# Norm factors by logarithm and exponential on ScalarE in place of GpSimd's power, and six buffers of routed rows for four

## What is computed

```python
def _layernorm(x, axis=-1, eps=1e-05):
    m = jnp.mean(x, axis=axis, keepdims=True)
    v = jnp.var(x, axis=axis, keepdims=True)
    return (x - m) / jnp.sqrt(v + eps)

x = _layernorm(x + attention(x, Wq, Wk, Wv, Wo, bo))   # 16 heads of 8, softmax
x = _layernorm(x + retention(x, ctx, ctx))             # decayed causal scores, rotated queries and keys, no softmax
x = _layernorm(x + experts(x, gate, w1, w2, w3))       # 8 experts of width 512, the two best by a softmax, silu(g) * u
```

## Time and profile before

| what | value |
|---|---|
| time, median of 3 runs | 1004.99 us (1000.88 to 1008.09) |
| the profiled execution | 1007.5 us |
| its span, first to last instruction | 1005.7 us |
| busy: PE, DVE, POOL, ACT | 804.7, 790.3, 652.6, 613.4 us |
| TensorE clock granted, mean | 0.915 |

### The profile page before, as it was taken

The page is one execution under the profiler, slowest core; times in us unless marked ns, Lnnn a source line. Parts: engine busy times, 40 slices in busy tenths (PEclk is TensorE's granted clock), DMA queues, the critical chain, the costliest instruction groups (busy, mean ns, idle before and its releaser), DMA issues.

```text
span 1005.7 us, 34508 instructions
## 1 busy us (share of the span) xinstructions
PE 804.7 (80%) x11940; PEld 603.2 (60%) x11940; DVE 790.3 (79%) x2155; ACT 613.4 (61%) x1416; POOL 652.6 (65%) x738
## 2 busy tenths in 40 slices
PE   1667799989999899898868660999999999999500
PEld 1345465656656556656544430799999999999500
DVE  4797799988999988998846644688888888888475
ACT  1133566768767777676666851676667666766355
POOL 0349767799999999998996456245444544454443
PEclk9788799999999999999987965899999999999855
DMA  9312222123232232221212004222222222222176
GB/s 307 81 29 54 40 48 50 42 62 70 51 71 62 54 74 52 61 58 42 63 39 62 23 22 91 58 61 66 63 62 61 66 63 61 62 65 58 53 252 226
DMA packets 145300, 72.55 MB, mean 72 GB/s; under 512 B 75024, under 2 KB 134544, under 8 KB 145136
## 3 DMA queue, kind: packets, MB, share of 16 engines
q1 hardware_dynamic: 124800, 40.43, 17.4%
q0 software_dynamic: 8640, 17.84, 5.4%
q10 hardware_dynamic: 11696, 12.08, 3.8%
HBM read 41.98 MB, written 28.34 MB: 70 GB/s over the span
## 4 chain that ended last, share of the span: by engine, by line
PE 38%; POOL 32%; issue 12%; DVE 3%; DMA 3%; ACT 2%; POOLq 0%; SPq 0%; ACTq 0%; DVEq 0%
POOL prod_ev L1536 17%; POOL routed_rows L1553 11%; PE QKV L773 9%; PE ST L773 9%; PE XT L801 6%; PE SC L801 5%; POOL rs L1516 3%; PE YY L589 2%; DMA prod_ev<-token_halves 2%; PE SC L560 1%; PE YY L791 1%; PE TR L791 1%; PE TR L606 1%; DMA routed_rows<-xe,pos 1%; PE TR L603 1%
## 5 line engine op out<-in xcount | busy, mean ns | idle before, releaser
L1536 POOL TENSOR_TENSOR prod_ev<-e_sb,q_v 128x512 f32<-128x512 f32 x256 | 300.2, 1206 | 70.5 <-PE YY L589 35.6
L1585 POOL DMA_INDIRECT token_halves<-w_new,tok_i x142 | 137.8, 971 | 32.5 <-issue 22.2
L1553 POOL DMA_INDIRECT routed_rows<-xe,pos x128 | 129.6, 1013 | 30.6 <-issue 29.9
L1151 DVE TENSOR_TENSOR prod_qk<-q_v,QKV 128x2048 f32<-128x2048 f32 x64 | 144.7, 2273 | 4.5 <-ACT q_v L870 4.5
L1438 DVE TENSOR_TENSOR prod_ev<-prod_qk,prod_ev 128x1024 f16<-128x1024 f32 x71 | 87.0, 1226 | 56.0 <-ACT prod_ev L1028 56.0
L1028 ACT CAST prod_ev<-prod_qk 128x1024 f16<-128x1024 f32 x71 | 74.2, 1045 | 76.0 <-DVE prod_qk L1464 51.4
L773 PE MATMUL QKV<-k_t,w_hl 128*128 128x256 f16 x852 | 116.8, 274 | 0.1
L773 PE MATMUL ST<-k_t,w_hl 128*128 128x256 f16 x852 | 116.7, 273 | 0.0
L409 POOL TENSOR_TENSOR marks<-half_c 128x1 f32<-128x1 f32 x103 | 19.9, 193 | 142.2 <-DVE w_new L1454 142.0
L1464 DVE SCALAR_TENSOR_TENSOR prod_qk<-ST,hid_scale,prod_qk 128x512 f32<-128x512 f32 x142 | 99.6, 744 | 2.3 <-ACT prod_qk L1037 2.3
L1037 ACT ACTIVATE prod_qk<-QKV,silu_scale 128x512 f32<-128x512 f32 x142 | 96.1, 678 | 8.6 <-PE QKV L773 4.6
(11 more groups left out here) (169 smaller groups left out, 1695.3 us busy)
## 6 DMA issues: line engine op xcount, KB each, us to landing
w_new<-routed_rows SPq DMA_DIRECT2D x71, 130.0 KB
prod_ev<-token_halves SPq DMA_DIRECT2D x16, 512.0 KB, 5.1
x_sb<-x SPq DMA_DIRECT2D x32, 128.0 KB, 3.0
x_res<-x SPq DMA_DIRECT2D x128, 32.0 KB
head_rows<-o_n SPq DMA_DIRECT2D x32, 128.0 KB
o_t<-head_rows SPq DMA_DIRECT2D x64, 64.0 KB
ctx_sb<-ctx SPq DMA_DIRECT2D x32, 128.0 KB, 2.7
out<-prod_qk ACTq DMA_DIRECT2D x16, 256.0 KB, 4.0
```

Source lines behind the costliest of these rows:

```text
L1151: eng.tensor_tensor(prod_qk[:, u, :, :].rearrange("p d (i j) -> p d i j", j=NH), q.unsqueeze(3).to_broadcast([P, HD, NH, NH]), k.unsqueeze ...
L1536: ins = eng.tensor_tensor(prod_ev[:, u, q, :, :, 0:HD], e_sb[:, it.slot(2), u, 64 * q:64 * q + 64].rearrange("p (i j) -> p j i", j=4).unsq ...
L1553: eng.indirect_dma_start(out=xs, out_offset=bass.IndirectOffsetOnAxis(ap=pos[:, r, 2 * u + k:2 * u + k + 1], axis=0), in_=xe[:, r, u, k, : ...
L1585: eng.indirect_dma_start(out=halves, out_offset=bass.IndirectOffsetOnAxis(ap=tok_i[:, s, u:u + 1], axis=0), in_=yw[:, s, u, :], in_offset= ...
```

## The change

- `one_over_std` moves from POOL to ACT. POOL's power and product go (L1516, L1527). ACT does three things in their place, between `row_ids(13)` and `blocks(9)`: ve = Ln(variance + eps), with eps as the bias, for 4 numbers a partition; rs = Exp(-0.5 * ve); and four one-column copies nb = nm * rs (each with a column of rs as its scale). Each of the three waits for the one before.
- DVE's `variances` loses its second instruction (variance + eps); nm now raises `nm_ready`, for which Ln waits.
- At the head of ACT's program, the activation table that holds both Ln and Exp is loaded.
- `xe` and the semaphores of the scatters have six homes (XE_RING) for four. `second_norm` and `gate_weights` wait for the scatter six duos back. `positions` still waits for the one four duos back, since `pos` keeps four buffers.

```diff
+XE_RING = 6
+def wait_row_ring(item, sems, back):
+    if item.off - back >= 0:
+        item.eng.wait_ge(sems[(item.off - back) % XE_RING], 64 * ((item.off - back) // XE_RING + 1))
...
-        xe = sb("xe", [RING, 2, 2, ROW])
+        xe = sb("xe", [XE_RING, 2, 2, ROW])
...
+            eng.preload_act_table_set("natural_log_exp_and_others")
             eng.wait_ge(tab_in, 16)
...
+            def one_over_std(c, d):
+
+                slot = norm_slot(c, d)
+                wait_norms(c, d, nm_ready)
+                eng.activation(ve[:, slot, :, :], mv[:, slot, :, :, 1], ACT.Ln, bias=eps_c[:, 0:1]).then_inc(ve_ready, 1)
+                wait_norms(c, d, ve_ready)
+                eng.activation(rs[:, slot, :, :].rearrange("p k u -> p (k u)"), ve[:, slot, :, :].rearrange("p k u -> p (k u)"),
+                               ACT.Exp, scale=-0.5).then_inc(rs_ready, 1)
+                wait_norms(c, d, rs_ready)
+                for k in range(2):
+                    for u in range(2):
+                        ins = eng.activation(nb[:, slot, k, u:u + 1], nm[:, slot, k, u:u + 1], ACT.Copy,
+                                             scale=rs[:, slot, k, u:u + 1])
+                ins.then_inc(nb_ready, 1)
...
                 wait(it, nb_ready, -NORM_GAP)
-                wait_ring(it, routed_out, RING, 64)
+                wait_row_ring(it, routed_out, XE_RING)
...
                 if it := at(13):
                     row_ids(it)
+                c, d = at(8), at(8 + NORM_GAP)
+                if c or d:
+                    one_over_std(c, d)
                 if it := at(9):
                     blocks(it)
...
-                eng.tensor_scalar(nm[:, slot, :, :], mv[:, slot, :, :, 0], -1.0, None, ALU.mult)
-                eng.tensor_scalar(ve[:, slot, :, :], mv[:, slot, :, :, 1], EPS, None, ALU.add).then_inc(ve_ready, 1)
+                eng.tensor_scalar(nm[:, slot, :, :], mv[:, slot, :, :, 0], -1.0, None, ALU.mult).then_inc(nm_ready, 1)
...
             def positions(it):
                 wait(it, posw_ready)
-                wait_ring(it, routed_out, RING, 64)
+                wait_row_ring(it, routed_out, RING)
...
-                eng.tensor_tensor(rs[:, slot, :, :].rearrange("p k u -> p (k u)"),
-                                  ve[:, slot, :, :].rearrange("p k u -> p (k u)"), half_c[:, 0:4], ALU.pow).then_inc(rs_ready, 1)
...
-                eng.tensor_tensor(nb[:, slot, :, :].rearrange("p k u -> p (k u)"), nm[:, slot, :, :].rearrange("p k u -> p (k u)"),
-                                  rs[:, slot, :, :].rearrange("p k u -> p (k u)"), ALU.mult).then_inc(nb_ready, 1)
...
                 if it := at(11):
                     scatter(it, 0)
-                c, d = at(5), at(5 + NORM_GAP)
-                if c or d:
-                    one_over_std(c, d)
-                c, d = at(5), at(5 + NORM_GAP)
-                if c or d:
-                    norm_shift(c, d)
                 if it := at(1):
                     weighted(it, 1, 0)
```

More of the change, by code:

```diff
@@ L377, in build @@
         ev_ready = [sem(f"ev_ready{u}") for u in range(2)]
-        ve_ready, rs_ready = sem("ve_ready"), sem("rs_ready")
-        x_in, ctx_in, routed_out = (ring_sem(n) for n in ("x_in", "ctx_in", "routed_out"))
+        nm_ready, ve_ready, rs_ready = sem("nm_ready"), sem("ve_ready"), sem("rs_ready")
+        x_in, ctx_in = (ring_sem(n) for n in ("x_in", "ctx_in"))
+        routed_out = [sem(f"routed_out{i}") for i in range(XE_RING)]
         y_in = ring_sem("y_in")
@@ L489, in _ @@
                               pad_rows[:, 2 * n:2 * n + 2, :]).then_inc(blank_out, 16)
-            for r in range(RING):
-                eng.wait_ge(routed_out[r], 64 * n_duo // RING)
+            for r in range(XE_RING):
+                eng.wait_ge(routed_out[r], 64 * ((n_duo - r + XE_RING - 1) // XE_RING))
             eng.wait_ge(blank_out, 16 + 16 * n_exp)
@@ L677, in rows_across @@
                 for u in range(2):
-                    mm = eng.transpose(X2T[:, P * u:P * u + P], xe[:, it.slot(RING), u, 0, 0:P], ident)
+                    mm = eng.transpose(X2T[:, P * u:P * u + P], xe[:, it.slot(XE_RING), u, 0, 0:P], ident)
                 mm.then_inc(x2t_done, 1)
@@ L853, in row_ids @@
                 wait(it, w1_ready)
-                eng.copy(xe[:, it.slot(RING), :, :, P + 1],
+                eng.copy(xe[:, it.slot(XE_RING), :, :, P + 1],
                                 const("ids")[:, bass.ds(it.number() * 4, 4)].rearrange("p (u k) -> p u k", k=2)
@@ L944, in second_norm @@
             def second_norm(it):
-                s, r, m = it.slot(2), it.slot(RING), norm_slot(None, it)
+                s, r, m = it.slot(2), it.slot(XE_RING), norm_slot(None, it)
                 wait(it, nb_ready, -NORM_GAP)
-                wait_ring(it, routed_out, RING, 64)
+                wait_row_ring(it, routed_out, XE_RING)
                 for u in range(2):
@@ L1286, in gate_weights @@
                 wait(it, dn_ready)
-                wait_ring(it, routed_out, RING, 64)
-                eng.reciprocal(xe[:, it.slot(RING), :, :, P], dn[:, it.slot(2), :, :]).then_inc(w1_ready, 1)
+                wait_row_ring(it, routed_out, XE_RING)
+                eng.reciprocal(xe[:, it.slot(XE_RING), :, :, P], dn[:, it.slot(2), :, :]).then_inc(w1_ready, 1)
             def places(it):
@@ L1544, in scatter @@
             def scatter(it, u):
-                r = it.slot(RING)
+                r, x = it.slot(RING), it.slot(XE_RING)
                 if u == 0:
@@ L1553, in scatter @@
                     eng.indirect_dma_start(out=xs, out_offset=bass.IndirectOffsetOnAxis(ap=pos[:, r, 2 * u + k:2 * u + k + 1], axis=0),
-                                           in_=xe[:, r, u, k, :], in_offset=None).then_inc(routed_out[r], 16)
+                                           in_=xe[:, x, u, k, :], in_offset=None).then_inc(routed_out[x], 16)
             def step(at):
```

## The result

The changed kernel took 1026.81 us at the median of 4 runs (1024.13 to 1029.21), the kernel before 1006.54 over 4 runs (1000.88 to 1010.2): ratio 1.0206, interval 1.0149 to 1.0262. The forecast was 972 in a range of 960 to 994, so it was wrong in sign. The profiled execution took 1024.13 us with a span of 1022.2, against 1005.7 before.

The account below looks back on a forecast made before the run. POOL was taken as the bound, 15.52 us in its best steps, with PE and DVE close behind. Gains of 22 (middle), 5 (fill), 3 (drain) and 3.3 (stage end) made 33.3 us, from 1004.99 to 972; range 960 to 994.

Parts of the forecast that it names:

- Where the stall goes: Middle steps: xq_a would fall among POOL's scatters, not its products, so its 0.97 us stall would be mostly gone.
- POOL's phase: Middle steps, counted from m_neg's end: POOL's products start at 1.4 us and its pair between the scatters at 8.6.
- It mends itself: Middle steps: if the stall returns, DVE and PE slow down, POOL gets ahead by the difference, and its pair ends sooner.
- Rival 3: Middle steps: one_hot and xq_a meet POOL's six products, 2.2 us more, a step of 16.4; 1016 us, chance 0.05.
- ACT's new work: ACT ahead of the first norm: Ln, Exp and four copies take 1.4 us, bounds 1.2 to 2.6, hidden by 1.66 idle.
- The fill: Stage A before 198.85: stalls of DVE's xq_a and one_hot go, gaining 5 us, bounds 0 and 9.
- The end: Stage A behind 512.80: 3 us from two more homes, 3.3 from last scatters no longer held behind the power.
- The step without a collision: Middle of stage A: 14.6 us a step for 15.70, bounds 14.3 and 15.2, gaining 22 us over 20 steps.
- rival 1: Middle steps: the collision at xq_a stays, a step of 15.2 and no gain in the fill; 989 us, chance 0.17.
- rival 2: ACT's six instructions cost 2.6 us, each drained before the next, a step of 15.4; 1000 us, chance 0.06.
- rival 4: ACT's tables for Ln and Exp replace each other, two loads of 1.28 us a step; 1023 us, chance 0.02.
- the rule on two-input instructions: POOL shares SBUF interfaces with DVE, with contention for two SBUF inputs; taken as giving no way to say which step meets which.

Follow-up runs that it names:

- e4: The changed kernel, with POOL's pair of products for u = 1 also waiting until DVE has written xk_b of the same step: 968.03 us, ratio 0.9624.
- e5: The changed kernel without Ln and Exp, rs a constant, the four small copies kept: 1025.35 us beside 1005.53, single run.
- e9: e4 without Ln and Exp, rs a constant written once: 963.7 us, single run.
- e1: The kernel before with six homes of xe alone, the power staying on POOL: 999.85 us beside 1006.44, ratio 0.9944.
- e2: The changed kernel with four homes in place of six, Ln, Exp and the copies staying on ACT: 1030.5 us, ratio 1.0242.
- e4b: The same kernel as e4, run again 5 times: 969.16 us beside 1005.13, ratio 0.9643.
- e8: The changed kernel with POOL's four scatters issued in a row and the pair of products behind them: 1053.54 us beside 1005.53, single run.
- e11: e4 with POOL's pair waiting for posf_ready, from the DVE instruction right ahead of xk_a, instead of xkb_ready: 1033.34 us beside 1009.22, single run.
- e3: The changed kernel with DVE's xk_a moved some 1.7 us earlier, directly behind its second large product: 1037.99 us, ratio 1.0323.
- e6: e4 with four homes of the routed rows in place of six: 980.32 us at the median of 6 runs, ratio 0.974 without the slowest.

## Why the prediction was wrong

**The step that failed: "Where the stall goes".** It took the two-input instructions that were held before, xq_a and one_hot, and placed them against POOL's cycle after the change. It didn't place the others, which were not held in the middle: xk_a had 417 ns there. That was no property of xk_a but one of the order, since the power's wait for ve kept the pair behind it. So the step was put at 14.6 and came out at 17.20, of which xk_a's hold is 2.76. In the steps shown the power didn't stand waiting (no bracket at 308.53 and 324.05), because POOL was late by its own work. The change took POOL's 1.28 us away, and with them the order. The traces could have told it. From m_neg's end (313.45), nm begins 8.7 later at 322.14, and the working had POOL's pair beginning at 8.6. And in the fill of the kernel before, xk_a had been held twice (1.19 and 1.01 us), the first time at the end of four products that ran from 97.07 to 101.62:

```profile
100.71 1.19 DVE L1191 TENSOR_TENSOR xk_a<-ctx_sb,tab 128x256 f32<-128x256 f32 x1
```

One thing they couldn't: xk_a, 8.0 to 8.4 after m_neg, would by the recorded times have been through before a pair at 8.6. That it was caught all the same is the early start of the hold, in the last section.

**POOL's phase was right to 0.1 us.** In the kernel after, m_neg's end is 322.79; the products begin at 324.29 (1.5 after, forecast 1.4) and the pair at 331.44 (8.65, forecast 8.6). xk_a begins at 330.79, that is 8.0 after. Both numbers count from the same m_neg, and they are the same in nearly every step of the middle (8.0 and 8.6), so the collision repeats.

**"It mends itself" was wrong for this place.** The argument was that a held DVE slows down PE, so that POOL's pair comes earlier relative to it. That needs a POOL that is late and can catch up. In the kernel after it isn't late: it waits in every step for PE's sums (2.98 us, above), which come after m_neg. xk_a stands behind the same m_neg that releases POOL: a hold of 2.8 us delays the next m_neg and with it POOL's next pair by as much, and nothing shifts the one against the other.

**The size of a hold.** Rival 3 had the right kind of mechanism, DVE's group on POOL's products, at the wrong place: xq_a and one_hot at the six products, with a step of 16.4 and 1016. It priced a hold by the mean excess of the fill, 0.5 and 0.86. Measured: in each step of the middle xk_a's hold lasts to the end of both products, 2.8 us. With that the step is 17.2, and the time 1027.

**What held.** ACT's new work was 1.33 us (317.29 to 318.62) for 1.4, and hidden: with all of it in place DVE waits for the first norm 1.1 us in 17 steps of e4 (xq_a's line there), and e5 and e9 show no gain in the middle without Ln and Exp, e9 with one_hot held. No table load came in the steps; ACT's trace has two in all (1.28 us each, at the heads of stages A and B), as before. ACT's waits for homes went. Stages B and C gave nothing, as said. The fill gave 4.9 for 5, in part by luck: xq_a's and one_hot's stalls did go, but nm, 0.16 to 0.17 us in the fill of before, was held there for 0.79 to 1.13 in its first six steps. The end gave 6.2 for 6.3, but not by the split of the forecast, which had 3 from the homes and 3.3 from the power that is gone: the homes alone give 7.3 there (e1), and the kernel after with four homes 0.5 (e2, 129.43 for 129.88). The step without a collision was forecast at 14.6, bounds 14.3 to 15.2; with POOL's wait given back it is 14.33, and the time 969 for 972. So the sum came near for a kernel with one more line in it, with the terms off in both directions: by e4b's trace the fill gave 2.6 for 5, 19 steps of the middle 26.3 for 21, and the end 10.0 for 6.3; that the total agrees so well is luck. Rivals 1, 2 and 4 didn't happen; rival 1's stall at xq_a went.

**By the Trainium skill**, SBUF — State Buffer, section "🔬 SBUF: two separate sides", the pair of ports that VectorE and GpSimd share is an exclusive lock, taken "for the whole instruction" by whichever of the two starts first. The prediction had weighed the rule on two-input instructions and left it without a duration. The traces agree that DVE is blocked and not slowed down: its held instructions end shortly behind POOL's products, xk_a by 0.30 us and nm by 0.04, however long they waited. They often show more than one instruction's length, however: a DVE instruction waited out two products in a row (2.29 us) here and four (4.52) in e8, where a single product is about 1.17. Not always: at 310.55 in the kernel before, one_hot's first half got in behind the first product of a pair (0.47 us), and in e11 nm did twice (0.80 at 281.67 and 387.51). What decides between the two I don't know.

## What to carry to other kernels

Before an instruction is taken off an engine, list what its waits kept in order, and not only what its time costs: an order that is hardly ever waited for in the middle leaves hardly a row there, and can be worth more than the work. Look for it in the fill, where the engine has the slack that the change will give it. When a change leaves an engine with slack that shares SBUF ports with DVE, compute the phase of each of its runs of products against every tensor_tensor and tensor_scalar of DVE that works from SBUF alone, those not held in the middle too, and ask whether both are released by the same event; if so, nothing here pulled them apart. A wait that holds the idle engine back until the group is through cost 2.5 us over 300 in e4b and bought 2.9 us a step.

## What the runs showed of the hardware

- A DVE tensor_scalar with one source is held as well. nm, 4 numbers a partition, takes 0.17 us when free and 2.0 at the mean in e3 and e11. By the Trainium skill, VectorE: DVE Perf Modes, section "Mode 2×_2P — use both read ports for one tensor", a one-source instruction from SBUF to SBUF may use both ports; the trace agrees in that it is held, and shows nothing of how it reads.
- By these two cases the hold begins when POOL's waits are over, ahead of the first product's own start: xk_a at 313.61 was held, though the pair is recorded from 314.24, while the second scatter still was being issued (313.27 to 314.22). In e11 xk_a began at 315.14, before the signal for which POOL's pair waited could come (posf ended at 315.23), and ran free; the pair is recorded from 315.77.
- POOL's issue of an indirect DMA held neither kind: xk_a at 315.14 in e11 lies beside a scatter with 0.42 us, and nm at 322.14 in the kernel before with 0.17.

Still open: the long steps of e6; what lets a held instruction in behind the first product and not the last; the 4 to 5 us of e9 in the drain, which rest on a single run; and why one run took 1354.83 us, with a granted clock of 0.559.
